# Second norm's mean and variance on VectorE, routing chain placed earlier in four instruction streams

## What is computed

```
h = _layernorm(x, axis=-1) * (1 + ca) + sa
x = x + ga * _L0_attn_ref(h, L0_attn_W_in, L0_attn_W_out)
h = _layernorm(x, axis=-1) * (1 + cb) + sb
x = x + gb * _L0_ffn_ref(h, routing_W, expert_bias, sW1, sb1, sW2, sb2, rW1, rb1, rW2, rb2)
...
# attention: 16 heads of 16; Chebyshev polynomials T0..T5 of clipped q and k
num = (Tq * beta * cumsum(Tk * v)).sum(orders);  den = (Tq.sum * beta * cumsum(Tk.sum)).sum(orders)
# experts: one shared and 8 routed, hidden 128
activation = sqrt(softplus(X @ routing_W.T + expert_bias)); top 2 of 8 -> combine
out = shared + sum_e combine[e] * (silu(X @ rW1[e] + rb1[e]) @ rW2[e] + rb2[e])
```

## Time and profile before

| | us |
|---|---|
| median of 3 runs (954.52 to 955.95) | 954.58 |
| the profiled execution | 953.07 |
| its span, first to last instruction | 951.3 |
| PE busy | 860.2 (90%) |
| DVE busy | 815.7 (86%) |
| ACT busy | 489.8 (51%) |
| POOL busy | 408.3 (43%) |

### The profile page before, as it was taken

One profiled execution on the slowest core, in us unless ns is written; L12 is line 12 of the kernel. 1 busy time (PEld: TensorE's weight loads), 2 busy tenths in 40 slices (PEclk: granted clock), 3 DMA queues, 4 the chain that ended last, 5 costly groups with the idle time before them and its releaser, 6 DMA issues. The chain is left out here.

```text
span 951.3 us, 14272 instructions
## 1 busy us (share of the span) xinstructions
PE 860.2 (90%) x4377; PEld 648.6 (68%) x4377; DVE 815.7 (86%) x1263; ACT 489.8 (51%) x860; POOL 408.3 (43%) x502
## 2 busy tenths in 40 slices
PE   5766739999999999999999999999999999979998
PEld 4545427676767676786767676777767676756786
DVE  2696979999989998999989998999999998889423
ACT  4634546555556656655656566566556563441321
POOL 2341444363636355453636254543646253463220
PEclk9975769999999999999999999999999999999999
DMA  8014134453533535453534445354634243443422
GB/s 309 1 29 89 45 68 145 86 153 76 137 92 77 153 79 160 86 155 70 153 77 96 130 87 165 68 155 90 162 71 133 66 100 113 78 133 83 117 79 55
DMA packets 51705, 100.34 MB, mean 105 GB/s; under 512 B 5380, under 2 KB 34127, under 8 KB 49623
## 3 DMA queue, kind: packets, MB, share of 16 engines
q1 hardware_dynamic: 36356, 66.14, 21.2%
q0 software_dynamic: 14832, 33.03, 20.2%
q10 hardware_dynamic: 482, 0.74, 0.2%
HBM read 57.68 MB, written 17.06 MB: 79 GB/s over the span
## 5 line engine op out<-in xcount | busy, mean ns | idle before, releaser
L1487 PE MATMUL acc<-w,hid 128*128 128x256 f32 x1128 | 262.5, 380 | 2.6 <-DVE hid L1169 2.6
L1487 PEld LDWEIGHTS acc<-w,hid 128*128 128x128 f32 x1128 | 213.9, 190 | 37.6 <-DVE hid L1169 4.7
L845 ACT ACTIVATE hid<-ring,b1row 128x512 f32<-128x512 f32 x144 | 98.7, 685 | 143.0 <-PE ring L1368 140.4
L1169 DVE TENSOR_TENSOR hid<-hid,cfw 128x512 f32<-128x512 f32 x128 | 111.1, 870 | 37.0 <-DMA cfw<-cf_rows 21.6
L665 POOL DMA_DIRECT2D feat<-feat x48 | 43.7, 910 | 228.8 <-DVE feat L1046 115.0
L800 ACT ACTIVATE feat<-ring,bqkv 128x512 f32<-128x512 f32 x96 | 65.7, 686 | 81.9 <-PE ring L1368 81.9
L1368 PE MATMUL ring<-n2H,w1H 128*128 128x512 f32 x288 | 102.5, 437 | 0.0
L1445 PE MATMUL tr<-wo_g,feat 128*128 128x256 f32 x256 | 65.3, 413 | 35.9 <-DVE feat L1088 35.9
L1021 DVE TENSOR_TENSOR_SCAN feat<-zero,carry,feat 128x512 f32<-128x512 f32 x80 | 97.1, 1261 | 0.0
L1021 DVE TENSOR_TENSOR_SCAN feat<-zero,feat 128x512 f32<-128x512 f32 x80 | 95.7, 1243 | 0.0
L1368 PE MATMUL ring<-n2H,w1L 128*128 128x512 f32 x288 | 90.8, 397 | 0.0
(11 more groups left out here) (171 smaller groups left out, 1559.8 us busy)
## 6 DMA issues: line engine op xcount, KB each, us to landing
feat<-feat POOLq DMA_DIRECT2D x48, 512.0 KB, 4.6
cfw<-cf_rows SPq DMA_DIRECT2D x16, 1280.0 KB, 7.6
xin<-in_L_attn_x SPq DMA_DIRECT2D x16, 512.0 KB, 9.3
feat<-inv_rows SPq DMA_DIRECT2D x32, 256.0 KB
cfw<-cf_rows SPq DMA_DIRECT2D x16, 512.0 KB, 3.6
out<-x SPq DMA_DIRECT2D x15, 512.0 KB, 8.5
out<-fin POOLq DMA_DIRECT2D x15, 512.0 KB, 6.0
cfw<-cf_rows SPq DMA_DIRECT2D x16, 256.0 KB, 4.5
```

The lines of the kernel that those rows point to most:

```text
L845: a.activation(hid[:, e % NG], ring[bank][:, :], ACT.Silu, bias=b1row[:, e:e + 1]).then_inc(ring_copied, 1)
L1169: v.tensor_tensor(hid[:, e % NG], hid[:, e % NG], cfw[:, (e - 1) % NW], ALU.mult).then_inc(hidw_ready, 1)
L1487: last = mm(acc[t // 2][:, t % 2], hid[:, e % NG, t * P:(t + 1) * P], w2[:, e], start=False, stop=(e == E), skip_group_check=True)
```

## The change

It changes no matmul and no attention instruction; it changes who computes the second norm's statistics, and the order in four streams.

- VectorE runs `second_mean_var` right behind the statistics: four BN_AGGR and two small TENSOR_SCALAR. GpSimd's `second_inv_std` has two instructions left of ten (power and product).
- GpSimd's `weigh_order_5` waits in addition for VectorE's second weighing (`weigh(i, p, 1)`).
- PE runs `transposes(0)` first in the step, behind each half of `residual`, and `transposes(1)`, `route_logits` and `logits_by_token` before `expert(1)`. `combine_by_expert` stands before `expert(8)`.
- VectorE: `lows(0)` stands before `odd`, `lows(1)` behind `expert(1)`, `logit_parts` behind `expert(3)`, `softplus` behind `expert(4)`, `combine_weights` before `den_key_sums`.
- ScalarE: `highs(0)` first, all of `normalise_second` between silu 0 and silu 1, `combine_rows` before the first norm of c+2. GpSimd: `exps` and `scores` before the second order sum, `split_weights` behind it.

```diff
+        def second_mean_var(dve, i, p):
+            c = number(i, p)
+            dve.wait_ge(stats_ready[1], c + 1)
+            dve.sem_inc(aggregate_begun, 1)
+            for t in range(NT):
+                last = nc.vector.bn_aggr(mean_var[:, t], stats[:, 1, t])
+            last.then_inc(aggregated, 1)
+            dve.wait_ge(aggregated, c + 1)
+            nc.vector.tensor_scalar(ms[:, 1, 8], mean_var[:, :, 1], EPS_LN, None, ALU.add).then_inc(mean_var_ready, 1)
+            nc.vector.tensor_scalar(ms[:, 1, 10], mean_var[:, :, 0], -1.0, None, ALU.mult).then_inc(mean_var_ready, 1)
+        def second_inv_std(pool, i, p):
+            c = number(i, p)
+            pool.wait_ge(mean_var_ready, 2 * c + 2)
+            ge(pool, norm_ready[1], c)
+            nc.gpsimd.tensor_tensor(ms[:, 1, 9], ms[:, 1, 8], k_("-half", NT), ALU.pow).then_inc(second_pow, 1)
+            pool.wait_ge(second_pow, c + 1)
+            nc.gpsimd.tensor_tensor(ms[:, 1, 11], ms[:, 1, 10], ms[:, 1, 9], ALU.mult).then_inc(rstd_ready[1], 1)
...
 (weigh_order_5)
                 ge(pool, numerator, c)
+                pool.wait_ge(weighted, (ND - 1) * c + 2)
                 g.tensor_tensor(f(W + 4), f(KT5), f(V0), ALU.mult).then_inc(weighted5, 1)
...
 (GpSimd step)
-                    inv_std(pool, 1, *later(i, p, -1))
+                    second_inv_std(pool, *later(i, p, -1))
...
                     token_means(pool, *later(i, p, 2))
+                if st["second"]:
+                    exps(*later(i, p, -1))
+                    scores(*later(i, p, -1))
                 if st["attn"]:
                     add_orders(i, p, 1)
+                if st["second"]:
+                    split_weights(*later(i, p, -1))
...
 (ScalarE step)
-                silu(0)
-                silu(1)
                 if qkv:
                     highs(0, *nxt)
+                silu(0)
+                if second:
+                    for t in range(NT):
+                        normalise_second(act, *prev, t)
+                silu(1)
                 silu(2)
                 if attn_:
                     scale_even(i, p)
-                for t, half in enumerate(HALVES[:4]):
-                    copy(half)
-                    if second:
-                        normalise_second(act, *prev, t)
-                silu(3)
                 if second:
                     highs(1, *prev)
-                silu(4)
+                for half in HALVES[:3]:
+                    copy(half)
                 if second:
                     copy_logits(*prev)
+                copy("q1")
+                silu(3)
+                silu(4)
...
                 silu(8)
+                if second:
+                    combine_rows(*prev)
...
 (VectorE step)
                     token_stats(dve, 1, *prev)
+                    second_mean_var(dve, *prev)
+                if qkv:
+                    lows(0, *nxt)
                 if attn_:
                     odd(i, p, 1)
                     weigh(i, p, 0)
-                if qkv:
-                    lows(0, *nxt)
-                if attn_:
                     weigh(i, p, 1)
                     prefix(i, p, 0)
...
                 expert(1)
+                if second:
+                    lows(1, *prev)
...
                 expert(3)
+                if second:
+                    logit_parts(*prev)
...
                 expert(4)
+                if second:
+                    softplus(*prev)
                 if attn_:
                     carry_over(i, p, 1)
                     order_product(i, p, 2)
                     order_product(i, p, 3)
                 if second:
-                    logit_parts(*prev)
+                    combine_weights(*prev)
...
 (TensorE transposes)
+                elif n:
+                    pe.wait_ge(x1_ready, 2 * (c + 1))
                 for k in range(KD):
+                    if n == 0:
+                        ge(pe, x1_ready, 2 * (c - 1) - 1 + k)
...
 (TensorE step)
+                if qkv:
+                    transposes(0, *nxt)
                 if ffn:
                     expert_up(*exp, use, 0)
                     expert_up(*exp, use, 1)
                     second_biases(*exp)
-                if qkv:
-                    transposes(0, *nxt)
                 expert(0)
-                if qkv:
-                    for half in HALVES[:4]:
-                        project(*nxt, use, half)
-                expert(1)
                 if second:
                     transposes(1, *prev, behind_norm=qkv)
-                expert(2)
+                if qkv:
+                    for half in HALVES[:3]:
+                        project(*nxt, use, half)
                 if second:
                     route_logits(*prev)
+                if qkv:
+                    project(*nxt, use, "q1")
+                if second:
+                    logits_by_token(*prev)
+                expert(1)
+                expert(2)
...
                 expert(7)
+                if second:
+                    combine_by_expert(*prev, attn_)
                 expert(8)
```

More of the change, by code:

```diff
@@ L136, in build @@
         stats = sb("stats", [P, 2, NT, 6])
+        mean_var = sb("mean_var", [P, NT, 2])
         ms = sb("ms", [P, 2, 12, NT])
@@ L223, in build @@
         var_steps = sem("variance_steps")
+        aggregate_begun, aggregated, mean_var_ready, second_pow = (
+            sem(f"second_{n}") for n in ("aggregate_begun", "aggregated", "mean_var", "pow"))
         sums_begun, squares_begun, norm_begun = (sem(f"{n}_begun") for n in ("token_sums", "token_squares", "normalisation"))
@@ L752, in step @@
                     token_means(pool, *later(i, p, 2))
+                if st["second"]:
+                    exps(*later(i, p, -1))
+                    scores(*later(i, p, -1))
                 if st["attn"]:
                     add_orders(i, p, 1)
+                if st["second"]:
+                    split_weights(*later(i, p, -1))
                 if st["norm"]:
                     inv_std_of_squares(pool, *later(i, p, 2))
-                if st["second"]:
-                    exps(*later(i, p, -1))
                 if st["attn"]:
                     add_orders(i, p, 2)
-                if st["second"]:
-                    scores(*later(i, p, -1))
-                    split_weights(*later(i, p, -1))
                 if st["ffn"] and not is_last(*later(i, p, -2)):
@@ L911, in step @@
                     row_biases(i, use if ffn else None)
-                if second:
-                    combine_rows(*prev)
             def high_weights():
@@ L1218, in step @@
                     prefix(i, p, 1)
-                if attn_:
                     carry_over(i, p, 0)
-                if second:
-                    lows(1, *prev)
-                if attn_:
                     order_product(i, p, 0)
@@ L1244, in step @@
                 expert(5)
-                if second:
-                    softplus(*prev)
                 if attn_:
@@ L1256, in step @@
                 expert(8)
-                if second:
-                    combine_weights(*prev)
                 if attn_:
@@ L1515, in expert @@
                             last_experts_by_bank(*exp)
+                if isinstance(i, int) and number(i, p) == 0:
+                    late_products_of_mods()
+                if qkv:
+                    transposes(0, *nxt)
                 if ffn:
@@ L1555, in step @@
                     project_out(i, p)
-                if second:
-                    combine_by_expert(*prev, attn_)
             def qkv_bias_products(ms):
```

7 lines of the change are left out of this document (removed).

## The result

| | before | changed |
|---|---|---|
| median, us | 954.55 (953.18 to 955.95, 4 runs) | 1039.03 (1035.78 to 1039.68, 4 runs) |
| profiled execution, span | 951.3 | 1037.3 |
| mean granted TensorE clock, share of full | 0.964 | 0.923 |

The ratio is 1.0878, 95% interval [1.0851, 1.0906]. Forecast were 965.5 and a range up to 974: the sign was right, the size wrong by more than 70 us.

What follows compares the result with a forecast made beforehand. PE and VectorE were taken to pass the bound to each other, the second norm's low part setting PE's 53.85 us step; 953.07 + 16.2 (six pairs) - 3.7 (ends) = 965.5 us, range 948 to 974.

Steps and rivals of the forecast that it cites:

- S to R: VectorE, projection's start (S) to residual's second half (R): output, two odd instructions, half a residual; 4.2 us.
- R to n2L: VectorE, from the residual's second half to the second norm's low part (n2L) ready, weighing stall included: 15.0 us.
- PE's waits: PE waits 3.05 us a step: about one at the first transposes, the rest at third projection's bank and logits.
- The step is 19.25 + 34.6: PE's step: 19.25 us up to the logits, then 34.6 us of PE work behind them; 53.85 us.
- The last order sum: GpSimd: split_weights, some 3 us, now precedes this DMA, which has about 1 us to spare; nothing charged.
- Moving `softplus` forward costs nothing in itself.: VectorE: the same engine does softplus before the inversion either way, so no cost was added.
- The ends: Program's ends: gain of 1 in step (0, 1), 2.7 in step (7, 1), 0 in last two; together -3.7 us.
- The sum: Whole program: 953.07 + 16.2 for six pairs of steps - 3.7 for the program's ends = 965.5 us.
- 1 (weighing behind n2L): GpSimd's fifth weighing slips behind the second norm's low part on VectorE; 944 to 956 us, centre 950; chance 0.26.
- 2 (the last product of `second_inv_std` starves): GpSimd misses three gaps behind lows(0), normalising ends 3.4 later; about 2 us a step, 977 us; chance 0.16.
- 3 (all waits vanish): Stretch before the second norm's low part as short as 12 us, step 51.8, program 939 us; chance 0.07.
- The last sentence of the prediction: If VectorE stands before the sum of the orders, the last order sum came late, which was priced at nothing.

Runs made afterwards that it cites:

- e7: Changed kernel with the routing chain behind the logits back in its old order; transposes, lows, highs and logits stay early: 977.94 us, ratio 1.024.
- e12: e7 with the routing logits, their transposes and their copy back behind the products of expert 2: 955.5 us, ratio 1.0007.
- e1: Changed kernel with GpSimd's split_weights behind the last order sum instead of before it: 999.98 us, ratio 1.0493.
- e11: Kernel before with two added unused power instructions of 1.04 us on GpSimd ahead of the last order sum: 985.35 us, ratio 1.0329.
- e3: Kernel before with the second norm's mean and variance on VectorE, no order changed: 950.32 us, ratio 0.9964.
- e2: Changed kernel without the new wait of GpSimd's fifth weighing on VectorE's second: 1035.64 us, ratio 1.0867.
- e9: Kernel before with four added unused power instructions of 1.04 us on GpSimd ahead of the last order sum: 1000.23 us, ratio 1.0471.

## Why the prediction was wrong

- **S to R, 4.2.** Right where the projection runs at full clock: from 619.67 to about 623.6, 3.9 us. With the projection at 6.57 us it is 6.7 (560.65 to 567.38). The term took the duration of the earlier trace rows for granted.
- **R to n2L, 15.0.** Right: 15.5 (567.38 to 582.87). Mean and variance took 0.66 (569.53 to 570.19) and 0.15 of waiting, against 0.68; the weighing's stall 2.1 (scans 4.56 instead of 2.45) against 2.15. By the Trainium skill, "VectorE: DVE Perf Modes", section on the TRN2 errata, six such instructions were an estimated 0.94; the trace has 0.81 with the wait, between that and my term.
- **PE's waits, 3.05 a step.** In e7 2.25. Right in kind. What failed is "The step is 19.25 + 34.6": the 34.6 us behind the logits were taken at full clock, and after a wait of 1.9 to 2.3 us they take 1.5 more. The same order without the early logits (e12) has no such wait, and its pair of steps is 105.51 (512.25 to 617.76), as before the change. With the front half (e7) the program takes 12.4 us more than the forecast for the whole change.
- **The last order sum.** This is the step that failed: "that DMA has to land before the division and has about 1 us to spare", priced at nothing. I compared some 3 us of new work with 1 us of room in the same sentence and did not subtract. It costs 39 us (e1), as a wait of 3 us a step and PE's cold projection behind it. The limit was also a different one. To its reader the sum had more room than I gave it: issued at 761.11 and landing 4.6 us later (the page's median), it was 3.6 us early for L1081 at 769.37. e11 used 1.4 of these, VectorE waited for the sum no more than before (4.5 us, once), and 31 us were lost all the same, at the inverse: the sum issued 2.1 us ahead of the inversion was harmless, at 0.8 ahead it was not.
- **"Moving `softplus` forward costs nothing in itself."** Wrong. It and `combine_weights`, with GpSimd's `exps` and `scores`, stand before the second order sum, the start of a chain with 5.1 us a link. In e1 the sums are 13.7 us apart (558.34 to 572.00), before 9.3. The work is the same, but what waits behind it is a DMA with a fixed length. As far as e1's trace shows, that and PE's wait for the late split are the 22 us from e7 to e1.
- **The ends, -3.7.** In e3 the wait of 4.21 is gone (845.08 there, no idle time), as forecast, and e3 gains 4 in all.
- **The sum.** 1039.0 is 73.5 us over the forecast: 12.4 up to e7, 22.0 to e1 and 39.1 from there. (The forecast's own terms add up to 965.6.)
- **Rivals.** 1 (weighing behind n2L) did not occur: the hold put it in the first scan. What the prediction cites of the Trainium skill, "SBUF — State Buffer", section "Who interferes with whom", is borne out by e2 as well: the weighing started at 566.19 and odd, behind it at 566.51, took 3.15 us. 2 (the last product of `second_inv_std` starves) did not occur: GpSimd's two instructions end at 571.6 and VectorE has n2L without a wait. 3 (all waits vanish) did not occur.

The last sentence of the prediction named the sign of what happened. The range ended below it because a term "priced at nothing" had no upper bound in it.

## What to carry to other kernels

Before work is moved ahead of a DMA on a queue, subtract: its room, less the moved work, and here the room ended some 2 us ahead of the next small round trip, not where the data is read. A transfer that adds what the one before has just written is a chain with a link of fixed length; find the gap between the two issues, and see what fills it already. When a forecast adds a wait of 2 us or more to TensorE, let the upper end of the range include the slow stretch behind it, from a row at the lower clock; here it followed such waits often, not always. And see beside which instructions of VectorE a long instruction of GpSimd will run: the same weighing cost 0.86 us in one place and 2.1 in another.

## What was not expected of the hardware

- The same 16 matmuls took 3.72 us at a granted clock of 1.00 and 6.57 at 0.56, after PE had stood for 1.29 and 3.31 us. Twelve matmuls of no use in front of them, in seven steps, gained 12 us of 1039. In e9 the projection took 3.72 us at 1.00 behind 3.36 us as well.
- From the inversion on, a round trip of 32 KB out and 512 KB in took 7.6 to 7.8 us when a 512 KB accumulating transfer on another queue had been issued 2.1 us ahead of the inversion, and up to 9.9 when it was issued within 1.2 us of it.
- An order sum took 4.6 us from issue to landing (the page's median over 48, below), and this length makes up most of the chain's link of 5.1. The Trainium skill, "SBUF — State Buffer", section "The DMA setup-cost knee", gives a fit of 2 us and the bytes by 436 GB/s for a transfer; for 512 KB that is an estimated 3.2 us. The trace disagrees for this accumulating transfer on GpSimd's queue, with 4.6.

```profile
feat<-feat POOLq DMA_DIRECT2D x48, 512.0 KB, 4.6
```
